# A transformer block on one core: pairs of score maxima moved between attention slots, gate products moved to slot 39

## Chip, cores and metric

The kernel runs on one core of a Trainium2 chip. The metric is the device time of one execution in microseconds (us); lower is better. Before the change the median of three runs is 2919.54 us.

## What is computed

The input is 8 images (batch entries) of 1024 tokens with 256 channels. Each goes through an attention part and a part with experts, both modulated by a vector per image:

```python
mod = (_silu(L0_c) @ L0_wmod).reshape(8, 6, 1, -1)
sa, ca, ga, sb, cb, gb = (mod[:, k] for k in range(6))      # gates ga, gb kept away from zero
h = _layernorm(x) * (1 + ca) + sa
x = x + ga * attn(h)     # 16 heads, causal, rope on 32 of 48 dimensions, output times W_o
h = _layernorm(x) * (1 + cb) + sb
x = x + gb * ffn(h)      # 16 experts of width 128 on 32-wide slices, top 2 of 16, then Wo and bo
```

In the attention, softmax of causal scores is taken for 16 heads; in the second part every token slice goes through all 16 experts and the gates of the top two weight their outputs, which are added and projected by Wo.

## The kernel before, in words

The work is written out by hand for each engine; instructions run in program order on each engine, and semaphores tie the engines together. An image has two stretches: 48 attention slots (`aslots`, index s), then 64 expert steps (`eslots`, index q). While an image attends, smaller pieces of work, called items, are put into its slots by `attend_slots`; while it goes through the experts, the first half of the next image's preparation is put into the steps by `expert_slots`.

A slot is one group of four heads g, one half c of the queries and one block j of 128 keys (`MAIN`). Heads go in two halves. PE (TensorE) computes scores of the first half, then the items of part 0 of the slot ("between"), then scores of the second half, then the items of parts 1 and 2 ("behind", "front"); at even slots it adds the product of weights and values of the two slots before (`values`). ScalarE takes the exponential of each half (L1393), and GpSimd masks the diagonal blocks (L1508). Scores of a half wait for the exponential two halves earlier. Slots on the diagonal are narrower: 512, 384, 256, 128 columns. In the second half of the queries four slots are full before those four. Slots 16 to 23 are diagonal ones of groups 2 and 3; 24 to 27, 32 to 35 and 40 to 43 are full.

Before the real scores of a group can be used, a maximum per row is needed. It comes from an item named ("pair", g, ...): two matmuls of up to 512 columns (L428, one for each half of the partitions; a masked pair is cut into four) into two PSUM banks, which VectorE reads with a masked maximum (L573, where the block lies on the diagonal) or a plain one (L576). There are 13 pairs for the second half of the queries of each group, 5 for the first. `rmax` (L582), `row` (transposed on PE at L500, copied by VectorE at L586) and a DMA of four issues on SyncE's queue (L780) carry the maximum to the queries of the group; the scores of a new group and half (slots 16, 20, 24, 32, 40) wait for it.

All items of PE write into a ring of three PSUM banks (`Ring`, banks 6, 7, 5): `ring_write` waits until the item that used the bank three uses before has been read. A pair takes two uses, a rope item, a group of transposes (`sums`, `tr`) or an output projection (`o`) takes one.

`PLACES` lists the places (slot, part) for the 47 pairs of a later image in order; slots 1, 2, 3, 5, 7 have one pair in part 0, from slot 9 to 36 an odd slot has one (part 0) and an even slot two (parts 0 and 1). The first image has its own list (`per_slot`). Eight rope items (rotary embedding of groups 2 and 3) lie in slots 0 and 2 to 8: VectorE shuffles (L607) and multiplies (L608), GpSimd multiplies and adds (L726, L739), SyncE moves the result to the queries and keys (L765).

In slot 22 VectorE forms the gated projections: `wog` = W_o times ga (two multiplications, L1474), `wfg` = Wo times gb (two, L1476), `bog` = bo times gb (L1478). The attention's output projection (`o`, L518, from slot 32 on) reads `wog` and waits for the semaphore d0_w. GpSimd adds `bog` to the residual at expert step 0; `wfg` is read by the last projection (`out`, L548) from expert step 36 on. The semaphore d0_w is cleared once an image.

Of the kernel before, what the change touches and what calls it, by code (L numbers as in the profile page):

```python
# [23 lines left out]
CH = C // P  # L24
# [312 lines left out]
PAIRS = [masked_pairs(0), [(((i, 0, pr),),) for i in range(4, 8) for pr in range(2)]]  # L337
# [74 lines left out]
def item_matmuls(pe, L, R, item):  # L412
# [57 lines left out]
    elif kind == "rope":  # L470
        g, isk, c = rope_of(item[1], R.alone)
        if g < 2:
            R.wait(pe, L, ("ht", c, CH - 1) if isk else ("qct", c))
        hd = slice(g * HG * RD, (g + 1) * HG * RD)
        if isk:
            for k in range(CH):
                mm = pe.matmul(out, L.wkr[:, k, hd], L.ht[:, k, half(c)], start=(k == 0), stop=(k == CH - 1))  # L477
        else:
            mm = pe.matmul(out, L.wqr[:, hd], L.qct[:, half(c)], start=True, stop=True)  # L479
    elif kind == "sum":  # L480
        R.wait(pe, L, ("kvt",))
        for t in range(4):
            mm = pe.matmul(out[:, 2 * t:2 * t + 2], L.kvsq[:, t * P:(t + 1) * P], L.halves[:, :], start=True, stop=True)
    elif kind == "qc":
        h, c = item[1:]
        R.wait(pe, L, ("qct", c))
        mm = pe.matmul(out, L.wqc[:, h * P:(h + 1) * P], L.qct[:, half(c)], start=True, stop=True)  # L487
    elif kind == "std":
        pe.wait_ge(S["f_ks"], 1)
        for t in range(4):  # L490
            for c in range(2):
                mm = pe.matmul(out[KVR * c:KVR * c + KVR, t * P:(t + 1) * P],
                               L.kstd[:, 4 * c + t:4 * c + t + 1].broadcast_to([P, KVR]), L.ident[:, :], start=True, stop=True)
    elif kind == "row":
        g, c = item[1:]
        if c:
            pe.wait_ge(S["c_mf"] if g else S["f_mf"], max(g, 1))
        else:
            R.wait(pe, L, ("pair", g, *PAIRS[0][-1]))
        mm = pe.transpose(out[0:4 * HG, 0:P], L.mxf if c else L.mx0[:, g, :], L.ident[:, :])  # L500
    elif kind == "sums":
        m = item[1]
        pe.wait_ge(S["c_o"], m + 1)
        for t in range(4):
            mm = pe.transpose(out[:, t * P:(t + 1) * P], L.ot[:, m % 2, t * P:(t + 1) * P], L.ident[:, :])  # L505
    elif kind == "tr":
        c, j = item[1:]
        R.wait(pe, L, ("sums", SEQ.index((NG - 1, c))))
        for t in range(4):
            mm = pe.transpose(out[:, t * P:(t + 1) * P], L.ao[:, 4 * c + t, j * P:(j + 1) * P], L.ident[:, :])  # L510
    elif kind == "o":
        c, n = item[1:]
        R.wait(pe, L, ("tr", c, CH - 1))
        if c == 0:
            pe.wait_ge(S["d0_w"], 5)
        for t in range(2):
            for k in range(CH):
                mm = pe.matmul(out[:, t * C:(t + 1) * C], L.at[:, k, (2 * n + t) * P:(2 * n + t + 1) * P], L.wog[:, k, :],  # L518
                               start=(k == 0), stop=(k == CH - 1))
    elif kind == "tr2":  # L520
        c, j = item[1:]
        pe.wait_ge(S[f"d{c}_xn"], 4)
        for t in range(4):
            mm = pe.transpose(out[:, t * P:(t + 1) * P], L.xn2[:, t, j * P:(j + 1) * P], L.ident[:, :])
    elif kind == "tm":
        c, j = item[1:]
        R.wait(pe, L, ("tr2", c, CH - 1))
        for k in range(CH):
            mm = pe.matmul(out, L.wms[:, k, j * P:(j + 1) * P], L.h2t[:, k, :], start=(k == 0), stop=(k == CH - 1))  # L529
    elif kind == "lg":  # L530
        c = item[1]
        R.wait(pe, L, ("tm", c, CH - 1))
        for t in range(4):
            for j in range(CH):
                o = t * P + j * 4 * NE
                mm = pe.matmul(out[:, o:o + 4 * NE], L.t32[:, j, t * P:(t + 1) * P], L.embd[:, :], start=True, stop=True)  # L536
    elif kind == "gt":
        c = item[1]
        pe.wait_ge(S[f"d{c}_r"], 17)
        for t in range(4):  # L540
            mm = pe.transpose(out[:, t * P:(t + 1) * P], L.eb[:, t * FH:(t + 1) * FH, :].rearrange("p a b -> p (a b)"),
                              L.ident[:, :])
    elif kind == "out":
        n = item[1]
        pe.wait_ge(S["e_add"], 30 * (n // 2 + 1))
        for t in range(2):
            for k in range(CH):
                mm = pe.matmul(out[:, t * C:(t + 1) * C], L.ct[:, k, (2 * n + t) * P:(2 * n + t + 1) * P], L.wfg[:, k, :],  # L548
                               start=(k == 0), stop=(k == CH - 1))
# [553 lines left out]

AHEAD = 2
EARLY = 3
PLACES = [(1, 0), (2, 0), (3, 0), (5, 0), (7, 0)]
PLACES += [(s, part) for s in range(9, 37) for part in range(2 - s % 2)]


def attend_slots(img):  # L1110


    slots = [([], [], []) for _ in range(NM)]
    if img:
        slots[1][1].extend([("out", 2), ("out", 3)])
        places = PLACES
        pairs = [("pair", 1, *p) for p in PAIRS[1][AHEAD:AHEAD + 5]]
        pairs += [("pair", g, *p) for g in (2, 3) for p in PAIRS[0]]
        pairs += [("pair", 1, *p) for p in PAIRS[1][AHEAD + 5:]]
        pairs += [("pair", g, *p) for g in (2, 3) for p in PAIRS[1]]  # L1120
    else:
        per_slot = [(0, 2), (1, 2), (2, 3), (3, 2), (4, 3), (5, 3), (8, 2), (9, 1), (10, 2), (11, 2), (12, 3), (13, 1), (14, 2), (15, 1),
                    (16, 2), (17, 2), (18, 2), (19, 1), (20, 2)] + [(s, 1 if s in (22, 23, 27, 29, 31, 33) else 2) for s in range(21, 37)]
        places = [(s, 2 * k // n) for s, n in per_slot for k in range(n)]
        early, second = [("pair", 0, *p) for p in PAIRS[1][EARLY:]], [("pair", 1, *p) for p in PAIRS[1]]
        pairs = early[:1] + [("pair", 1, *p) for p in PAIRS[0]] + early[1:]
        pairs += second[:5] + [("pair", 2, *p) for p in PAIRS[0]] + second[5:6] + [("pair", 3, *p) for p in PAIRS[0]] + second[6:]
        pairs += [("pair", g, *p) for g in (2, 3) for p in PAIRS[1]]
        slots[2][1].append(("row", 1, 0))
        slots[6][0].append(("rmax", 0))  # L1130
        slots[6][1].append(("row", 0, 1))
    assert len(places) == len(pairs)
    ropes = {s: ("rope", 8 + k) for k, s in enumerate((0, 2, 3, 4, 5, 6, 7, 8) if img else (3, 5, 6, 7, 8, 9, 10, 11))}
    for (s, part), pair in zip(places, pairs):
        if part and img and s and s in ropes:
            slots[s][1].append(ropes.pop(s))
        slots[s][part].append(pair)
    for s, rope in ropes.items():
        slots[s][1].append(rope)
    for s, g in ((21, 1), (29, 2), (37, 3)):  # L1140
        slots[s][0].insert(0, ("rmax", g))
    for s, row in ((13, (2, 0)), (17, (3, 0)), (21, (1, 1)), (29, (2, 1)), (37, (3, 1))):
        slots[s][2].append(("row", *row))
    for m, gc in enumerate(SEQ[:-1]):
        last = max(s for s, step in enumerate(MAIN) if step[:2] == gc)
        slots[last + 2][2].append(("sums", m))
    slots[27][1].append(("tr", 0, 0))
    slots[28][1].append(("tr", 0, 1))
    slots[32][1].append(("o", 0, 0))
    slots[33][1].extend([("o", 0, 1), ("stats", 0)])  # L1150
    slots[34][1].append(("xn", 0))
    slots[37][1].extend([("tr2", 0, 0), ("tr2", 0, 1)])
    slots[38][1].append(("tm", 0, 0))
    slots[39][1].extend([("tm", 0, 1), ("tlo", 0, 0)])
    slots[40][1].extend([("tlo", 0, 1), ("lg", 0), ("chain", 0, 1), ("chain", 0, 2)])
    slots[41][1].append(("exp", 0))
    for k in range(3, 18):
        slots[41 + (k - 3) // 3][1].append(("chain", 0, k))
    slots[46][2].append(("gt", 0))
    return slots  # L1160
# [68 lines left out]
def all_images(nc, L, O):  # L1229
# [18 lines left out]
    with nc.Block() as block:  # L1248
# [182 lines left out]
        def _(v):  # L1431
# [29 lines left out]
            for img in range(B):  # L1461
                for s, (between, behind, front) in enumerate(aslots[img]):
# [6 lines left out]
                    if s == 22:  # L1469
# [3 lines left out]
                        for k in range(CH):  # L1473
                            v.tensor_tensor(L.wog[:, k, :], L.wos[:, k, :], L.gate[:, 0, :],  # L1474
                                            ALU.mult).then_inc(S["d0_w"], 1)
                            v.tensor_tensor(L.wfg[:, k, :], L.wfs[:, k, :], L.gate[:, 1, :],  # L1476
                                            ALU.mult).then_inc(S["d0_w"], 1)
                        v.tensor_tensor(L.bog[:, :], L.bor[:, :], L.gate[:, 1, :], ALU.mult).then_inc(S["d0_w"], 1)  # L1478
# [214 lines left out]
```

## Time and profile before

| | us |
|---|---|
| runs of the kernel, median (lowest to highest) | 2919.54 (2918.32 to 2922.02) |
| the profiled execution, its own time | 2920.5 |
| its span, first to last instruction | 2918.1 |
| PE busy | 2816.6 |
| VectorE busy | 1863.0 |
| ScalarE busy | 1808.5 |
| GpSimd busy | 1246.2 |

The profile is one execution. PE is a matmul's stretch, PEld a weight load, DVE is VectorE, ACT ScalarE, POOL GpSimd, SPq the queue of DMA issues of SyncE. L428 is line 428 of the kernel. A busy time is the union of the instructions' stretches; matmuls overlap each other, so a stretch of matmuls is best read from start to start. "[0.45 <-DVE front L573]" behind an instruction tells that its engine was idle 0.45 us before it and that an update by VectorE's instruction of line 573 ended that.

### The profile page before, as it was taken

The numbers are of one execution on the slowest core, as the hardware profiler recorded it, in microseconds if no ns is written. First come the engines' busy times: TensorE is split into PE (matmuls) and PEld (weight loads), VectorE is DVE, ScalarE is ACT, GpSimd is POOL, SyncE is SP. The second block draws the span as 40 slices with busy tenths as digits, with TensorE's granted clock in tenths as the row PEclk, the third lists the DMA queues.
The fourth block names the chain that finished last, engine by engine and source line by source line (L and its number), as shares of the span: only waits on it lengthen the run. The fifth ranks groups of instructions, "written<-read, shape, count | busy, mean of one in ns | idle before, by whom it ended". The sixth has DMA issues, their size and how long they took to land.

```text
span 2918.1 us, 50109 instructions
## 1 busy us (share of the span) xinstructions
PE 2816.6 (97%) x16476; PEld 1241.9 (43%) x16476; DVE 1863.0 (64%) x4638; ACT 1808.5 (62%) x2148; POOL 1246.2 (43%) x1325
## 2 busy tenths in 40 slices
PE   7899999999999999999999999999999999999999
PEld 3344444444444443444444444444444444444433
DVE  5775666756666666666667666675756657667553
ACT  2346675566755677457675576655666566665687
POOL 4312645136451364414654146531565215561254
PEclk9899999999999999999999999999999999999999
DMA  6203453044430444304432055311453124530343
GB/s 156 57 5 99 118 130 73 1 108 122 120 71 8 119 118 107 71 21 121 122 97 61 23 134 130 87 47 46 121 133 89 32 71 119 124 88 20 77 127 94
DMA packets 176972, 252.96 MB, mean 87 GB/s; under 512 B 50509, under 2 KB 83293, under 8 KB 176621
## 3 DMA queue, kind: packets, MB, share of 16 engines
q1 hardware_dynamic: 176100, 248.44, 34.3%
q8 instruction: 136, 2.23, 0.3%
q10 hardware_dynamic: 620, 1.34, 0.2%
q14 instruction: 116, 0.95, 0.1%
HBM read 159.13 MB, written 12.63 MB: 59 GB/s over the span
## 4 chain that ended last, share of the span: by engine, by line
PE 86%; DVE 7%; issue 3%; ACT 2%; POOL 1%; SPq 1%; DMA 1%; ACTq 0%; DVEq 0%; POOLq 0%
PE ps L1279 17%; PE ps L1321 17%; PE ps L1339 16%; PE ps L1305 9%; PE ps L428 7%; PE ps L477 4%; PE ps L479 2%; PE ps L518 2%; PE ps L548 2%; DVE rest L573 1%; PE ps L529 1%; PE ps L505 1%; PE ps L536 1%; PE ps L463 1%; PE ps L487 1%
## 5 line engine op out<-in xcount | busy, mean ns | idle before, releaser
L1411 ACT ACTIVATE rest<-ps 128x1024 f32<-128x1024 f32 x1024 | 993.8, 1024 | 341.1 <-PE ps L1321 340.9
L1393 ACT ACTIVATE rest<-ps 128x1024 f32<-128x1024 f32 (+3 forms) x768 | 610.2, 809 | 537.4 <-PE ps L1279 511.6
L1518 POOL TENSOR_TENSOR rest<-rest 128x512 f32<-128x512 f32 x478 | 632.0, 1322 | 560.7 <-DVE rest L1448 548.1
L1448 DVE SCALAR_TENSOR_TENSOR rest<-ps,b2c,wide 128x512 f32<-128x512 f32 x512 | 384.0, 750 | 489.8 <-PE ps L1339 451.7
L1321 PE MATMUL ps<-wide,w1s 98*128 98x512 f32 x2048 | 655.1, 437 | 11.5 <-ACT rest L1411 8.7
L1339 PE MATMUL ps<-rest,w2s 128*32 128x512 f32 x4096 | 546.1, 605 | 0.6 <-ACT rest L1411 0.6
L1508 POOL TENSOR_SCALAR_AFFINE_SELECT rest<-rest 128x256 f32<-128x256 f32 x512 | 206.4, 411 | 772.3 <-ACT rest L1393 770.3
L573 DVE CUSTOM_DVE_ANT_0 rest<-ps,maskd 128x512 f32<-128x512 f32 (+3 forms) x1024 | 444.8, 487 | 118.8 <-PE ps L428 114.0
L1279 PE MATMUL ps<-wide 49*128 49x512 f32 (+3 forms) x2304 | 486.3, 511 | 10.2 <-ACT rest L1393 4.2
L1321 PEld LDWEIGHTS ps<-wide,w1s 98*128 98x128 f32 x2048 | 340.8, 188 | 301.0 <-ACT rest L1411 189.0
L576 DVE TENSOR_REDUCE front<-ps 128x1 f32<-128x512 f32 x512 | 329.0, 684 | 92.9 <-PE ps L428 88.7
L428 PE MATMUL ps<-wide 48*128 48x512 f32 (+3 forms) x1152 | 269.9, 500 | 37.8 <-DVE front L573 20.7
L1305 PE MATMUL ps<-rest,front 128*32 128x512 f32 (+3 forms) x3072 | 290.2, 496 | 0.0
L1279 PEld LDWEIGHTS ps<-wide 49*128 49x128 f32 x2304 | 195.5, 186 | 195.7 <-issue 121.3
L726 POOL TENSOR_TENSOR front<-front,sin 128x512 f32<-128x512 f32 x128 | 163.7, 1279 | 110.5 <-DVE front L607 110.2
L428 PEld LDWEIGHTS ps<-wide 48*128 48x128 f32 x1152 | 108.0, 187 | 219.1 <-DVE front L573 79.1
L1279 PE MATMUL ps<-heads 49*128 49x512 f32 (+3 forms) x768 | 168.0, 520 | 2.8 <-DMA heads<-front 2.6
L739 POOL TENSOR_TENSOR front<-front 128x512 f32<-128x512 f32 x128 | 163.0, 1273 | 10.0
L1339 PEld LDWEIGHTS ps<-rest,w2s 128*32 128x32 f32 x4096 | 80.6, 108 | 191.0 <-issue 189.5
L1305 PEld LDWEIGHTS ps<-rest,front 128*32 128x32 f32 x3072 | 80.7, 110 | 163.0 <-issue 113.5
L477 PE MATMUL ps<-front,wkr 128*128 128x512 f32 x256 | 125.5, 619 | 0.0
L1279 PEld LDWEIGHTS ps<-heads 49*128 49x128 f32 x768 | 66.7, 191 | 66.0 <-issue 43.8
(142 smaller groups left out, 2192.4 us busy)
## 6 DMA issues: line engine op xcount, KB each, us to landing
wide<-gate_rows SPq DMA_DIRECT2D x1024, 128.0 KB, 2.8
wide<-front SPq DMA_DIRECT2D x480, 64.0 KB, 2.0
wide<-front SPq DMA_DIRECT2D x192, 128.0 KB, 2.3
ao<-in_x SPq DMA_DIRECT2D x16, 512.0 KB, 5.1
heads<-front SPq DMA_DIRECT2D x64, 128.0 KB, 2.3
xs<-in_x SPq DMA_DIRECT2D x16, 512.0 KB, 5.0
out<-xs SPq DMA_DIRECT2D x32, 256.0 KB, 2.7
wide<-ao SPq DMA_DIRECT2D x96, 64.0 KB, 2.3
```

The costliest lines, as they stand in the source:

```text
L428: mm = pe.matmul(outs[hh][:, at:at + w], L.q2[g][rows, pr, i * P:(i + 1) * P].bitcast(F32R), L.k2[g][rows, pr, keys].bitcast(F32R), start= ...
L477: mm = pe.matmul(out, L.wkr[:, k, hd], L.ht[:, k, half(c)], start=(k == 0), stop=(k == CH - 1))
L573: ins = v.tensor_tensor_reduce(out=R.junk[hh][:, at:at + w], in0=src[:, at:at + w], in1=L.maskd[:, HALF - w:], scale=1.0, scalar=-3e38, op ...
L576: ins = v.tensor_reduce(dst, src[:, 0:w], AX.X, ALU.max)
L1279: mm = pe.matmul(bank(2 * (u % 2) + hh)[:, 0:HALF - f], L.k2[g][rows, pr, j * P:(j + 1) * P], L.q2[g][rows, pr, c * HALF + f:(c + 1) * HAL ...
L1305: mm = pe.matmul(bank(PVB)[h * VW:(h + 1) * VW, f:HALF], L.va[:, j, HG * g + h, :], L.pt[:, u % PTS, h % 2, f:HALF], start=(j == 0), stop= ...
L1321: mm = pe.matmul(bank(2 * (u % 2) + k), L.w1s[:, e, :], L.x2[:, c, 4 * j + 2 * p + k, :], start=True, stop=True)
L1339: mm = pe.matmul(bank(L2 + q % 2)[FD * h:FD * h + FD, :], L.w2s[:, e, :], L.hm[:, (2 * q + h // 2) % HM, (h % 2) * HALF:(h % 2 + 1) * HALF ...
L1393: nc.scalar.activation(L.pt[:, u % PTS, :, f:HALF], L.ps[:, 2 * (u % 2):2 * (u % 2) + 2, 0:HALF - f], ACT.Exp, scale=SCALE).then_inc(S["c_ ...
L1411: nc.scalar.activation(L.hm[:, u % HM, :], bank(2 * (u % 2), 2), ACT.Gelu).then_inc(S["e_gelu"], 1)
L1448: v.scalar_tensor_tensor(out=dst, in0=bank(L2 + q % 2), scalar=L.b2c[:, e:e + 1], in1=L.gb[:, q // 2 % GB, q % 2, :], op0=ALU.add, op1=ALU ...
L1518: g.tensor_tensor(dst, dst, L.gy[:, k % GY, :], ALU.add).then_inc(S["e_add"], 1)
```

## The change

Three things are changed. In the table of places for later images one pair less stands in slots 18, 22, 24 and 34 (each loses the one in part 1), and one more in slots 4 and 8 (part 0, where none stood) and in 27 and 35 (part 1, behind the one in part 0). So that the two new early places can be filled before the keys of group 2 are there, seven pairs of group 1 go first instead of five. The order of pairs within a group stays, the number is 47 as before. Second, three of the five gate multiplications (`wfg`, `bog`) move from slot 22 to behind the items of slot 39, for all images. Third, PE's wait before the first attention projection asks for two multiplications instead of five.

```diff
@@ -512,7 +512,7 @@
         if c == 0:
-            pe.wait_ge(S["d0_w"], 5)
+            pe.wait_ge(S["d0_w"], CH)
@@ -1103,8 +1103,9 @@
 AHEAD = 2
 EARLY = 3
-PLACES = [(1, 0), (2, 0), (3, 0), (5, 0), (7, 0)]
-PLACES += [(s, part) for s in range(9, 37) for part in range(2 - s % 2)]
+SOON = 7
+PLACES = [(s, 0) for s in (1, 2, 3, 4, 5, 7, 8)]
+PLACES += [(s, part) for s in range(9, 37) for part in range(2 - (s % 2 or s in (18, 22, 24, 34)) + (s in (27, 35)))]
@@ -1114,9 +1115,9 @@
-        pairs = [("pair", 1, *p) for p in PAIRS[1][AHEAD:AHEAD + 5]]
+        pairs = [("pair", 1, *p) for p in PAIRS[1][AHEAD:AHEAD + SOON]]
         pairs += [("pair", g, *p) for g in (2, 3) for p in PAIRS[0]]
-        pairs += [("pair", 1, *p) for p in PAIRS[1][AHEAD + 5:]]
+        pairs += [("pair", 1, *p) for p in PAIRS[1][AHEAD + SOON:]]
@@ -1473,6 +1474,8 @@
                         for k in range(CH):
                             v.tensor_tensor(L.wog[:, k, :], L.wos[:, k, :], L.gate[:, 0, :],
                                             ALU.mult).then_inc(S["d0_w"], 1)
+                    if s == 39:
+                        for k in range(CH):
                             v.tensor_tensor(L.wfg[:, k, :], L.wfs[:, k, :], L.gate[:, 1, :],
                                             ALU.mult).then_inc(S["d0_w"], 1)
                         v.tensor_tensor(L.bog[:, :], L.bor[:, :], L.gate[:, 1, :], ALU.mult).then_inc(S["d0_w"], 1)
```

## Rows read from the trace of the kernel before

**Rows 1.** The page: span, busy time of each engine, chain by engine.

```profile
span 2918.1 us, 50109 instructions
...
PE 2816.6 (97%) x16476; PEld 1241.9 (43%) x16476; DVE 1863.0 (64%) x4638; ACT 1808.5 (62%) x2148; POOL 1246.2 (43%) x1325
...
PE 86%; DVE 7%; issue 3%; ACT 2%; POOL 1%; SPq 1%; DMA 1%; ACTq 0%; DVEq 0%; POOLq 0%
```

**Rows 2.** Windows: window, length, busy per engine (count), clock, DMA; third image's attention.

```profile
807.50:968.50 161.00, 156.11 (x1018) 70.68 (x1018) 104.63 (x299) 85.88 (x112) 48.60 (x82) 1.00 0.19 44
```

**Rows 3.** Windows: slots 4, 17, 18, 21, 22, 24, 26, 27, 34, 35, 42.

```profile
823.78:828.40 4.62, 4.62 (x30) 1.78 (x29) 1.97 (x6) 1.94 (x2) 3.26 (x4) 1.00 0.28 70
867.93:870.45 2.52, 2.52 (x20) 1.39 (x16) 1.93 (x5) 2.07 (x3) 0.74 (x2) 1.00 0.00 0
870.45:874.34 3.89, 3.44 (x30) 1.52 (x29) 3.39 (x9) 1.33 (x3) 1.22 (x3) 1.00 0.01 2
878.83:881.48 2.65, 2.64 (x21) 1.48 (x18) 2.08 (x11) 2.15 (x3) 0.74 (x2) 1.00 0.03 6
881.48:885.41 3.93, 3.50 (x31) 1.62 (x31) 3.68 (x16) 1.26 (x3) 1.22 (x3) 1.00 0.02 4
886.48:890.60 4.12, 3.71 (x31) 1.50 (x31) 4.06 (x14) 2.36 (x3) 0.98 (x2) 1.00 0.00 0
893.34:897.87 4.53, 4.52 (x30) 1.52 (x29) 3.28 (x8) 2.60 (x3) 0.00 (x0) 1.00 0.00 0
897.87:900.61 2.74, 2.74 (x19) 1.30 (x15) 1.29 (x2) 1.49 (x2) 0.00 (x0) 1.00 0.00 0
922.96:928.38 5.42, 4.50 (x29) 1.51 (x29) 5.24 (x18) 2.05 (x2) 1.02 (x1) 1.00 0.00 0
928.38:930.63 2.25, 2.23 (x14) 0.88 (x10) 1.66 (x6) 1.02 (x1) 0.00 (x0) 1.00 0.00 0
952.23:956.00 3.77, 3.77 (x26) 1.10 (x25) 3.63 (x7) 3.06 (x4) 0.00 (x0) 1.00 0.40 94
```

**Rows 4.** Timeline, slot 18: start, us, engine, line, [idle before <-releaser].

```profile
872.03 0.69 DVE L573 CUSTOM_DVE_ANT_0 rest<-ps,maskd 128x512 f32<-128x512 f32 x1
...
872.26 0.50 PE L428 MATMUL ps<-wide 48*128 48x512 f32 x2 [0.45 <-DVE front L573]
```

**Rows 5.** Chain, slots 22 to 24: first and last gate piece of five, and next.

```profile
885.31 0.34 DVE rest L1474
...
886.65 0.54 DVE rest L1478
887.20 0.61 DVE front L576
```

**Rows 6.** Timeline, PE in slots 24, 26 and 27.

```profile
889.81 0.86 PE L1305 MATMUL ps<-rest,front 128*32 128x256 f32 x16
...
894.54 1.02 PE L1279 MATMUL ps<-wide 49*128 49x512 f32 x4
...
895.58 0.51 PE L428 MATMUL ps<-wide 48*128 48x512 f32 x2
...
896.01 1.92 PE L1305 MATMUL ps<-rest,front 128*32 128x512 f32 x16
...
899.07 1.02 PE L1279 MATMUL ps<-wide 49*128 49x512 f32 x4
...
900.02 0.66 PE L510 MATMUL ps<-ident,ao 128*128 128x128 f32 x4
```

**Rows 7.** Timeline, VectorE's first instruction after slot 39.

```profile
946.57 0.69 DVE L661 TENSOR_TENSOR front<-front 128x512 fp32r<-128x512 f32 x1 [3.51 <-ACT front L697]
```

**Rows 8.** Timeline, issues of the score row of slot 21.

```profile
881.75 2.42 SPq L780 DMA_DIRECT2D wide<-front  x4
```

**Rows 9.** The page, DMA issues: KB each, us from issue to landing.

```profile
wide<-front SPq DMA_DIRECT2D x480, 64.0 KB, 2.0
```

**Rows 10.** Timeline: load behind the last rope move; first pair of group 3.

```profile
848.06 1.19 SPq L1563 DMA_DIRECT2D xs<-in_x  x2
...
854.75 0.56 PE L428 MATMUL ps<-wide 48*128 48x128 f32 x4
```

## The prediction, made before the changed kernel ran

> **What bounds the kernel now.** I read the page first, then the attention stretch in windows, then single slots. The page gives TensorE (PE) 97% busy and 86% of the chain that ended last, VectorE 7% of that chain [rows 1]. So the end is set by the matmul queue, and whatever holds that queue for a moment is paid in full. The seven later images repeat each other: each has 48 attention slots in 161.0 us, and in the windows of all seven that length and PE's busy time agree within 0.1 us [rows 2]. I therefore cost one image (the third, from 807.5 us) and multiply by seven. In these 161.0 us PE is busy 156.1, so 4.9 us per image are plain idle time, and the granted clock there is 1.00, the level of 2.4 GHz [rows 2]. The windows by slot show where that idle time lies: slots 18, 22, 24 and 34 have 3.89-3.44 = 0.45, 3.93-3.50 = 0.43, 4.12-3.71 = 0.41 and 5.42-4.50 = 0.92 us, together 2.21 of 4.9; slots 4, 26, 27 have none to speak of [rows 3]. What ends it is VectorE: the second pair of slot 18 starts at 872.26 after 0.45 us idle that ended with L573, VectorE's masked maximum of the slot's first pair [rows 4]. A pair takes two of three PSUM banks, so the next pair must wait until VectorE has read the bank written three uses before. In slot 24 the pair waits behind more than that: the chain runs through the five gate multiplications, from 885.31 to the end of the last at 887.20, before the maximum that frees the bank [rows 5].
>
> **Price of a pair on PE.** The start-to-start times of the timeline give two prices [rows 6]. A second pair (behind both scores): in slot 26, scores at 894.54, pair at 895.58, values at 896.01, that is 1.47; the same scores without a second pair take 900.02-899.07 = 0.95; so 0.52. A first pair (between the two scores): in slot 27 scores, pair, scores take 900.02-897.87 = 2.15, where slot 27 starts at 897.87 [rows 3]; slot 42, with no pair, takes 3.77 in all, of which its two value groups of full width take what they take in slot 26, 897.87-896.01 = 1.86, leaving 1.91; so 0.24. A pair between the scores costs less than half of one behind them.
>
> **Part by part, one later image.**
> - Slot 18, second pair out: the idle 0.45 and the pair's 0.52 go: -0.97. What is late next is ScalarE's exponential of slot 17, already there before. Slot 22 likewise: -(0.43+0.52) = -0.95.
> - Slot 24: with one pair it is slot 27's 2.15 plus its own value groups, 890.60-889.81 = 0.79 [rows 3, 6], so 2.94 for 4.12: -1.18. More than 0.41+0.52, because here the first pair is held by the gate multiplications, and part of that hides in modelled matmul ends.
> - Slot 34: slot 42's 3.77 plus a first pair 0.24 is 4.01 for 5.42: -1.41.
> - Slot 21 now gets an unmasked pair where it had a masked one that held the transposes behind it. Slot 17, the same shape, takes 2.52 for 2.65 [rows 3]; between 0 and -0.13, I take -0.08, as VectorE still reads the pair just before.
> - Slots 4 and 8 get a first pair each: +0.24 each. VectorE has room: it is busy 1.97 of 4.62 us there [rows 3], a pair needs about 1.3 to 1.4 of it, and both sit ahead of that slot's rope item, whose data come later anyway. If that cover is gone, the rope turn on GpSimd (3.26 of 4.62 busy) is late, see the rivals.
> - Slot 27 gets a second pair: +0.52, and its first is now masked (a little longer on VectorE) with transposes behind the second, which wait for the first one's banks: I add 0.08. Lower bound 0.44 (the pair's own matmuls), upper bound the price it had in slot 34, 5.42-4.01 = 1.41. I take 0.60, as nothing else stands on VectorE in slots 26 and 27 (3.28 of 4.53 and 1.29 of 2.74 busy), which is slot 26's case, not slot 34's.
> - Slot 35 gets a second pair: +0.52, less the 0.10 by which it now waits for an exponential (2.25 against slot 27's 2.15): +0.42, same upper bound. Slot 36 then starts with VectorE still on that pair: +0.10, between 0 and 0.3.
> - Gates: two multiplications stay in slot 22 (0.34 each from start to start [rows 5]), three move behind slot 39's items. There VectorE is idle 3.51 us up to 946.57 [rows 7], and they need about 1.2. The first reader of what they write is GpSimd at the first expert step, eight slots on. The wait for two instead of five counts lets L518 go earlier, but it is passed long before slot 32. Hidden: 0.
> - Order within each group of heads is the same, so slots 16, 19, 20, 23, 25, 26, 28 to 33 keep their lengths, 0 +- 0.1 in all.
> - Score rows by DMA: a shorter slot 22 brings slot 24 forward to 881.48+(3.93-0.95)+1.07 = 885.53. Its row's four issues begin at 881.75 and last 2.42, the fourth starting near 883.6 [rows 8]; no row shows when these 2 KB writes land. Nearest, small writes on the same queue: 2.0 us [rows 9], so 885.6: a wait of 0.07. Below, 0; above, the old start 886.48, since it was met. Slot 20 has about 0.1 more room. I take 0.05.
> - The first image has its own table of places; only the gates move there, in a slot without a second pair: 0 to -0.3, I take 0.
>
> Sum: -0.97-0.95-1.18-1.41-0.08 = -4.59; +0.24+0.24+0.60+0.42+0.10+0.05 = +1.65; -2.94 an image, -20.6 us for seven. The profiled span 2918.1 becomes 2897.5 (the execution's own time 2920.5 becomes 2899.9, 2.4 of it outside the span); the median of the runs is 1.4 above the span, so 2919.5-20.6 = 2898.9 us.
>
> The 97% above could be read as "hardly anything to win". The Trainium skill, Perfetto Trace Analysis, Identifying the Most-Contended Engine, says that matmul busy time is a poor measure because matmuls are pipelined. The trace agrees: counted in idle time alone the four slots hold 2.21 us, counted from start to start 4.51. With idle time alone the sum would be 2.21 less the four added pairs' 1.55, seven times 0.7, near 2915 us.
>
> **Rivals.**
> 1. The stalls move instead of going: the second pairs in 27 and 35 are held as slot 34's was, 1.41 each. For: the same three banks, and VectorE busy 5.24 of 5.42 in slot 34. Against: that was slot 34's statistics and sums, which 27 and 35 do not have. Then +1.81 more, -1.1 an image: 2912.
> 2. The DMA of the score rows becomes the bound: slots 20 and 24 cannot start before they did. For: the margin is below 0.2 us by the nearest row. Against: it takes a landing of 2.9 us after the fourth issue. Then 0.97+0.95+0.08 are lost, -0.94 an image: 2913.
> 3. Slower: the pairs in slots 4 and 8 delay the rope items, hence GpSimd's turns, and the keys of head group 3 reach their place late; PE's first pair of that group, at 854.75 in slot 12, waits, with all behind it. In the trace the last of those issues is over by 848.06, when the next load starts on the queue [rows 10]; with about 2 us to land there are some 5 us of room. It decides from 5 us of lateness, and makes the kernel slower only from 8; 9 us would give +1 an image, 2927. Two pairs of 1.4 on VectorE can hardly give that.
> 4. The change does not do what it says: were the removed pairs' time not freed at all, slower by seven times 1.6; the rows of slot 18 speak against it, since the idle time before the pair ends with VectorE's read and nothing else.
>
> **How the numbers follow.** Forecast 0.84, rival 1 0.06, rival 2 0.05, rivals 3 and 4 together 0.03, a mixture near no change 0.02. The forecast's own bounds are -3.5 (slot 27 at its lower end, no DMA wait, slot 21 at -0.13, small gains in the first image and in slots 16 to 33) and -2.0 an image (one of the two added second pairs held for most of its 0.9 more): 2895 to 2906. Rivals 1 and 2 lie above that and are left out, 0.14 with the others, and a little at the ends. Measurement tells this kernel from no change at about 0.2%, 5.8 us, or 0.83 an image; all cases but the last two pass it. Faster 0.94, same 0.03, slower 0.03.
>
> **What would show it.** Per later image the attention stretch should fall from 161.0 to about 158.1 and the expert stretch stay. Slots 18 and 22 near 2.9 to 3.0, slot 24 near 2.95, slot 34 near 4.0; slots 4 and 8 near 4.86, 27 near 3.35, 35 near 2.67. The gate multiplications L1476 and L1478 lie in slot 39 without a wait behind them. Wrong would be: idle time of PE before the second pair in 27 or 35; the first score of slot 24 released by a DMA; a first pair in slot 4 that costs 0.5; or a slot 12 that waits for the rope move.

## The result, and the profile after

The changed kernel takes 2896.7 us, the median of five runs (2896.62 to 2899.86), against 2919.54 for the kernel before (five runs, 2916.97 to 2922.02); the ratio is 0.9924, 95% interval 0.991 to 0.9939. The forecast was 2898.9 in a range of 2895.0 to 2906.0, faster with a chance of 0.94. The profiled execution of the changed kernel is its slowest run: 2899.86 us, with a span of 2898.0. The page has the same counts of instructions as before, and a chain in which VectorE's share has gone from 7% to 5% [rows 1].

```profile
span 2898.0 us, 50109 instructions
...
PE 2809.7 (97%) x16476; PEld 1241.3 (43%) x16476; DVE 1864.4 (64%) x4638; ACT 1811.2 (62%) x2148; POOL 1248.8 (43%) x1325
...
PE 87%; DVE 5%; issue 3%; ACT 2%; POOL 1%; SPq 1%; DMA 1%; ACTq 0%; DVEq 0%; POOLq 0%
```

The windows of the third image show where the time went (same columns as [rows 2, 3]). First its whole attention stretch, then slots 4, 18, 21, 22, 24, 27, 34, 35 and 36.

```profile
808.40:966.45 158.05, 155.24 (x1018) 70.69 (x1018) 104.71 (x299) 86.15 (x112) 48.79 (x82) 1.00 0.19 45
...
824.63:829.49 4.86, 4.86 (x32) 1.98 (x31) 3.25 (x8) 2.05 (x2) 3.27 (x4) 1.00 0.31 80
871.84:874.78 2.94, 2.94 (x28) 1.30 (x27) 2.08 (x5) 1.33 (x3) 1.23 (x3) 1.00 0.01 2
879.31:881.82 2.51, 2.51 (x19) 1.39 (x15) 2.19 (x10) 2.06 (x3) 0.71 (x2) 1.00 0.03 7
881.82:884.82 3.00, 3.00 (x30) 1.40 (x29) 2.77 (x13) 1.34 (x3) 1.23 (x3) 1.00 0.02 5
885.88:888.83 2.95, 2.95 (x28) 1.41 (x29) 2.45 (x10) 2.02 (x3) 0.74 (x2) 1.00 0.00 0
896.10:899.45 3.35, 3.32 (x20) 1.52 (x16) 1.91 (x5) 2.05 (x2) 0.00 (x0) 1.00 0.00 0
921.82:925.83 4.01, 4.01 (x27) 1.30 (x26) 3.87 (x16) 2.05 (x2) 1.02 (x1) 1.00 0.00 0
925.83:928.38 2.55, 2.54 (x17) 1.21 (x15) 2.04 (x5) 1.30 (x2) 0.00 (x0) 1.00 0.00 0
928.38:933.05 4.67, 4.67 (x30) 1.40 (x26) 4.21 (x10) 2.80 (x3) 0.82 (x2) 1.00 0.00 0
```

Slots 18, 22, 24 and 34 now have their whole length as PE's busy time; the idle 0.45, 0.43, 0.41 and 0.92 us of before are gone. The table has the medians over the seven later images.

| slot | before, us | after, us | difference | forecast |
|---|---|---|---|---|
| 4, 8 (each) | 4.62 | 4.86 | +0.24 | +0.24 |
| 18 | 3.89 | 2.94 | -0.95 | -0.97 |
| 20 | 3.42 | 3.47 | +0.05 | 0 |
| 21 | 2.65 | 2.52 | -0.13 | -0.08 |
| 22 | 3.93 | 2.99 | -0.94 | -0.95 |
| 24 | 4.12 | 2.95 | -1.17 | -1.18 |
| 27 | 2.74 | 3.35 | +0.61 | +0.60 |
| 34 | 5.42 | 4.01 | -1.41 | -1.41 |
| 35 | 2.25 | 2.54 | +0.29 | +0.42 |
| 36 | 4.50 | 4.67 | +0.17 | +0.10 |

Together with hundredths elsewhere the attention stretch is 3.02 us shorter in each later image (161.00 to 157.98; forecast 2.94), the expert stretches between them keep their 194.45 us. Seven times 3.02 is 21.1; the spans differ by 20.1. The missing 1.0 us is not in the later images' attention or in the expert stretches between them, but in the first image's attention, the last expert stretch and the start. The rows of the changed kernel for the first two:

```profile
61.20:261.40 200.20, 175.10 (x1039) 77.10 (x1039) 130.64 (x382) 85.72 (x111) 49.03 (x81) 0.89 0.18 41
...
2728.60:2898.00 169.40, 160.31 (x880) 64.39 (x880) 78.08 (x110) 132.48 (x140) 82.98 (x63) 1.00 0.45 117
```

Before, the same two took 195.6 us at a granted clock of 0.91 and 172.3 us at 0.98, and the first began at 62.0 instead of 61.2 us. So the first image was 4.6 longer at a lower clock, the last stretch 2.9 shorter at 1.00, the start 0.8 shorter. A clock below 1.00 is a part of the stretch at 1.2 GHz instead of 2.4. Over all profiled kernels of this study but one the first image took 194.4 to 200.2 us, and over all of them the last expert stretch 169.4 to 174.0, with no relation to the edit that could be seen. (The exception is the kernel with half reads below, whose edit reaches the first image too: 187.8 us.) The times of one kernel scatter by 3 to 8 us (thirteen runs of the kernel before: 2914.86 to 2921.13), while a later image of the kernel before repeats within 0.02 us and one of the changed kernel within 0.12. The comparisons below are made per later image where they can be.

### The profile page after: what moved, and what is told of

Its sections match the earlier page's. It is cut to its first block, busy times and chain, and to the rows that moved or that the text cites. A ratio compares the mean times of both kernels' runs of the same rounds, so it can differ in the third digit from the quotient of the medians.

```text
span 2898.0 us, 50109 instructions
## 1 busy us (share of the span) xinstructions
PE 2809.7 (97%) x16476; PEld 1241.3 (43%) x16476; DVE 1864.4 (64%) x4638; ACT 1811.2 (62%) x2148; POOL 1248.8 (43%) x1325
## 4 chain that ended last, share of the span: by engine, by line
PE 87%; DVE 5%; issue 3%; ACT 2%; POOL 1%; SPq 1%; DMA 1%; ACTq 0%; DVEq 0%; POOLq 0%
PE ps L1280 18%; PE ps L1322 17%; PE ps L1340 16%; PE ps L1306 9%; PE ps L428 7%; PE ps L477 4%; PE ps L479 2%; PE ps L548 2%; PE ps L518 2%; PE ps L529 1%; PE ps L505 1%; PE ps L536 1%; PE ps L463 1%; PE ps L487 1%; DVE rest L1449 1%
```

## Experiments

Prices below are medians over the seven later images, from windows of the same kind, and "an image" is the sum of the slots' medians. In the diffs the lines with a minus are those of the kernel that was edited; "..." stands for lines left out. A kernel that ran once only has no interval; its windows still hold seven later images.

**The gate products alone.** Places of before, gates as changed.

```diff
-SOON = 7
-PLACES = [(s, 0) for s in (1, 2, 3, 4, 5, 7, 8)]
-PLACES += [(s, part) for s in range(9, 37) for part in range(2 - (s % 2 or s in (18, 22, 24, 34)) + (s in (27, 35)))]
+SOON = 5
+PLACES = [(1, 0), (2, 0), (3, 0), (5, 0), (7, 0)]
+PLACES += [(s, part) for s in range(9, 37) for part in range(2 - s % 2)]
```

> The kernel before with the three gate multiplications (wfg, bog) moved from slot 22 to slot 39 and the places of the pairs left as they were. Theory A (the stalls come from the ring of three banks behind VectorE, and each slot can be priced alone): only slot 24 changes. VectorE is through with the two wog multiplications 1.2 us earlier, the first pair of slot 24 finds its banks free, and slot 24 takes 3.5 us instead of 4.12; slots 18, 22 and 34 keep 3.89, 3.93 and 5.42. That is -0.6 us a later image, -4 us in all, about 2915. Rival B (the gate work on VectorE is most of the gain, the places add little): slots 22 and 24 fall to about 3.0 each, -2 us an image, -14 us in all, about 2905.

Ten runs gave 2916.68 against 2917.89 us for the kernel before, ratio 0.9996 (0.9986 to 1.0005). Only slot 24 changed, 4.12 to 3.51, and an image got 0.60 shorter, as expected. Its window:

```profile
885.33:888.84 3.51, 3.44 (x31) 1.62 (x31) 3.12 (x12) 2.36 (x3) 0.74 (x2) 1.00 0.00 0
```

Seven times 0.6 is 4.2 us, less than the scatter of single runs; the windows see it, the whole time does not tell it from nothing. The window confirms that the three products sat ahead of the reads on which slot 24's pairs wait [rows 5].

**The places alone.** Everything as changed, but all five products in slot 22.

```diff
-                    if s == 39:
+                    if s == 22:
```

> The changed kernel with all five gate multiplications back in slot 22. Theory A: slots 18, 22, 34 as in the changed kernel (2.94, 2.99, 4.01); VectorE ends the gate work 4.3 us after the start of slot 22, that is 1.3 us into slot 23, so the pair of slot 23 is read 0.55 us later, the first pair of slot 24 waits a little and slot 24 takes about 3.05 to 3.15 instead of 2.95. Gain 2.9 us an image instead of 3.0, about 2898. So gates alone and places alone add up to more than both together. Rival B: the gate work holds slot 24 at about 4.1 and slot 23 with it, and 1.2 us an image of the gain are lost, about 2905.

2898.6 us, ratio 0.9935 (0.9919 to 0.9952), -3.01 an image: the same as the whole change. The expected loss did not come. Slot 24 is as short as with the gates moved:

```profile
883.26:886.20 2.94, 2.94 (x28) 1.29 (x28) 2.77 (x11) 2.01 (x3) 0.78 (x2) 1.00 0.00 0
```

The first pair does start later, 0.85 us into the slot instead of 0.54 in the changed kernel, as the products still stand before the reads. But from its start to the second scores it then takes 0.32 instead of 0.64, and these begin 1.17 us into the slot, no later than the 1.18 of the changed kernel:

```profile
884.11 0.51 PE L428 MATMUL ps<-wide 48*128 48x256 f32 x4
...
884.43 1.06 PE L1280 MATMUL ps<-wide 49*128 49x512 f32 x4
```

With one pair in the slot, a first pair that is this late is absorbed. So the two parts do not add: alone the gates are worth 0.60 and the places 3.01, together 3.02. Moving the gate products is worth nothing in this kernel once slot 24's second pair is gone.

**One pair from slot 34 to slot 35, nothing else.**

```diff
-PLACES += [(s, part) for s in range(9, 37) for part in range(2 - s % 2)]
+PLACES += [(s, part) for s in range(9, 37) for part in range(2 - (s % 2 or s == 34) + (s == 35))]
```

> The kernel before with one move alone: the second pair of slot 34 goes to slot 35. Theory A: slot 34 falls from 5.42 to 4.01, slot 35 rises from 2.25 to 2.54 and slot 36 from 4.50 to 4.68; nothing else changes. -0.94 us a later image, -6.6 us in all, span about 2911. Rival C (the vector engine's total work in slots 34 to 36 sets their length, wherever the pair stands): the three slots keep their sum of 12.17 and the span stays at 2918.

One run: 2910.98 us, -0.96 an image where -0.94 was expected. Slots 34, 35 and 36:

```profile
921.28:925.28 4.00, 4.00 (x27) 1.29 (x26) 3.86 (x16) 2.05 (x2) 1.02 (x1) 1.00 0.00 0
925.28:927.82 2.54, 2.53 (x16) 1.21 (x14) 2.04 (x5) 1.29 (x2) 0.00 (x0) 1.00 0.00 0
927.82:932.50 4.68, 4.68 (x31) 1.40 (x27) 4.22 (x10) 2.81 (x3) 0.82 (x2) 1.00 0.00 0
```

This one move carries its own third of the gain, and the pair that lost 1.41 in slot 34 costs 0.29 + 0.17 = 0.46 in its new place. For this pair rival 1, stalls that move along, is false; for the one moved to slot 27 the window of the changed kernel says the same (+0.61, not 1.41).

**What a second pair's 0.52 consists of.** In the kernel before, VectorE reads only the first 256 of 512 columns of each pair that is unmasked or lies in a single block, and so leaves the other half of the keys out of these maxima. PE's instructions and their order are unchanged.

```diff
+                r = HALF // 2 if w == HALF and R.rope0 else w
...
-                    ins = v.tensor_tensor_reduce(out=R.junk[hh][:, at:at + w], in0=src[:, at:at + w], in1=L.maskd[:, HALF - w:], scale=1.0,
+                    ins = v.tensor_tensor_reduce(out=R.junk[hh][:, at:at + r], in0=src[:, at:at + r], in1=L.maskd[:, HALF - r:], scale=1.0,
...
-                    ins = v.tensor_reduce(dst, src[:, 0:w], AX.X, ALU.max)
+                    ins = v.tensor_reduce(dst, src[:, 0:r], AX.X, ALU.max)
```

> The kernel before, in which VectorE reads only the first 256 of the 512 columns of an unmasked or single-block pair in the later ring of every image (the maxima over the other half of the keys are left out). PE's instructions and their order are the same; such a read takes about 0.42 us instead of 0.69. Theory A (the bank read by VectorE holds the second pair): slot 18 from 3.89 to 3.62, slot 22 from 3.93 to 3.66, slot 34 from 5.42 to 5.15, slot 24 from 4.12 to about 3.5, each by the 0.27 us that the read of the first bank is shorter (slot 24 by two such reads before it). Rival D (a second pair costs PE itself more, by its weight loads or the change between forms of matmul, and VectorE's update only happens to come then): the slots keep their lengths. Only the stalls can change: slots 26 and 27, where the second pair or none is held, keep 4.53 and 2.74.

2885.87 us in one run, -3.41 an image. The two reads of a pair fell from 1.29 to 0.76 us, 0.27 each, and slots 18, 22 and 34 fell by 0.27 each as expected (slots 18, 24, 26 and 34 below; before in [rows 3]). But slot 24 fell by 0.27 too, where 0.6 was expected, and slots that should have stood still did not: 12, 16, 20 and 36 by 0.26, 28, 32 and 30 by 0.34, 0.31 and 0.21, 17 by 0.14, and slot 26 from 4.52 to 4.25, though PE was shown busy for all but 0.01 us of it [rows 3].

```profile
857.75:861.37 3.62, 3.45 (x30) 1.52 (x29) 2.21 (x8) 1.47 (x3) 1.22 (x3) 1.00 0.01 2
872.98:876.83 3.85, 3.71 (x30) 1.50 (x30) 3.52 (x14) 2.37 (x3) 0.98 (x2) 1.00 0.00 0
879.58:883.83 4.25, 4.25 (x30) 1.51 (x29) 2.22 (x8) 2.60 (x3) 0.00 (x0) 1.00 0.00 0
908.05:913.20 5.15, 4.50 (x30) 1.51 (x29) 4.71 (x20) 2.05 (x2) 1.02 (x1) 1.00 0.00 0
```

The timeline of slot 26 with half reads shows where the 0.27 was; PE's partners of before are in [rows 6].

```profile
880.78 1.02 PE L1280 MATMUL ps<-wide 49*128 49x512 f32 x4
881.55 0.49 PE L428 MATMUL ps<-wide 48*128 48x512 f32 x2
881.97 1.92 PE L1306 MATMUL ps<-rest,front 128*32 128x512 f32 x16
...
880.97 0.76 DVE L577 TENSOR_REDUCE front<-ps 128x1 f32<-128x256 f32 x2 [0.57 <-PE ps L428]
```

VectorE's two reads of the first pair in the kernel before:

```profile
894.74 1.29 DVE L576 TENSOR_REDUCE front<-ps 128x1 f32<-128x512 f32 x2 [0.57 <-PE ps L428]
```

Before, the second pair started 895.58 - 894.54 = 1.04 us after the scores ahead of it; now it starts 881.55 - 880.78 = 0.77 after them. In both, that is some 0.2 us after VectorE's first read ends (880.97 and half of 0.76, 881.35, here; 894.74 and half of 1.29, 895.38, before). The time was a wait for the bank, and no idle time was shown, because the scores' stretch of 1.02 us covers it: here that stretch would end at 881.80, 0.25 after the pair behind it began. The Trainium skill, Perfetto Trace Analysis, Tensor Engine Instruction, says that a matmul's end in the profile is computed and not observed; this row agrees, and shows what follows from it: a wait of up to a quarter of a microsecond leaves no gap.

So the 0.52 of the second pair in slot 26 was at least 0.27 of waiting for VectorE. Even with the shorter read the pair still starts 0.2 us after that read ends, so the 0.25 that is left is an upper bound for its matmuls; it is about what a first pair costs (0.24). Of the other even slots with a second pair, 10 and 14 kept their length; the rest fell by 0.21 to 0.34.

**Following that further: pairs into slot 6.** If a first pair costs 0.24 and a second pair in 14 and 30 still 1.0 and 0.87, slots 14 and 30 should be emptied as well, into slots 6 and 25.

```diff
-SOON = 7
-PLACES = [(s, 0) for s in (1, 2, 3, 4, 5, 7, 8)]
-PLACES += [(s, part) for s in range(9, 37) for part in range(2 - (s % 2 or s in (18, 22, 24, 34)) + (s in (27, 35)))]
+SOON = 8
+PLACES = [(s, 0) for s in range(1, 9)]
+PLACES += [(s, part) for s in range(9, 37) for part in range(2 - (s % 2 or s in (14, 18, 22, 24, 30, 34)) + (s in (25, 27, 35)))]
```

> The changed kernel with two more moves by the same prices: a first pair in slot 6 (none there) for the second pair of slot 14, and a second pair in slot 25 for that of slot 30; eight pairs of the first group go ahead. Theory A: slot 6 +0.24, slot 14 from 4.37 to about 3.3 (its second pair is held by VectorE for 0.6 and costs 0.43 itself), slot 25 +0.6, slot 30 from 4.26 to about 3.25. Together -1.2 us a later image against the changed kernel, -8 us in all, about 2889. Rival C: what is freed in slots 14 and 30 comes back as waits in the next narrow slots or, since slot 6 lies among the rope items with GpSimd nearly full, as a late rope move at slots 9 to 12: no change against the changed kernel, 2897.

2900.47 us, ratio 0.9943 (0.9928 to 0.9958), so not better than the change. Slots 14 and 30 fell to 3.37, by 1.00 and 0.86, and 25 rose by 0.59, as expected. Slot 6 rose from 3.76 to 4.69, by 0.93 instead of 0.24, and slot 15 by 0.13 in the median, as slot 16 behind it waits for its score row (in three of the seven images by 0.5 to 0.8). Slot 6, with what the pair waits for:

```profile
827.02:831.71 4.69, 4.27 (x30) 1.56 (x29) 4.17 (x9) 1.19 (x2) 4.24 (x6) 1.00 0.51 112
...
827.32 0.68 DVE L608 TENSOR_TENSOR front<-ps,cos 128x512 f32<-128x512 f32 x1
828.15 0.50 PE L428 MATMUL ps<-wide 48*128 48x512 f32 x2 [0.42 <-DVE front L608]
```

The pair's second bank is still held by the rope item of slot 5, whose multiplication ends at 828.00; the transposes of slot 5 took the use between them. A place in the ring costs what the item three uses before makes of it, not what the slot looks like.

**The same with slot 6's pair behind the scores.**

```diff
-PLACES = [(s, 0) for s in range(1, 9)]
+PLACES = [(1, 0), (2, 0), (3, 0), (4, 0), (5, 0), (6, 1), (7, 0), (8, 0)]
```

> The changed kernel with the moves out of slots 14 and 30 again (one into slot 25), but the early pair in slot 6 stands behind the rope item instead of between the scores. Between the scores it cost 0.93 us, since its second bank is the one that VectorE reads for slot 5's rope item until 0.98 us into slot 6. Theory A: behind, at about 2.1 us, that bank is long free and it costs its plain price, slot 6 from 3.76 to about 4.25; slot 14 to 3.37, slot 15 to 1.2 (the row of slot 13 now lands after slot 16 could start), slot 25 to 3.33 and slot 30 to 3.37 as in the run before. -0.6 us a later image against the changed kernel, about 2893. Rival C: GpSimd's rope work or the rows take it back, 2897.

2896.79 us, ratio 0.9924 (0.9907 to 0.9941). Slot 6 came to 4.18, +0.42 over 3.76:

```profile
833.27:837.45 4.18, 4.18 (x29) 1.58 (x28) 3.51 (x9) 1.08 (x2) 3.88 (x6) 1.00 0.57 125
```

The medians of the slots add up to -0.60 an image against the change, as expected, but the attention stretches of its images now vary from 157.33 to 158.18, with a mean of only -0.34 an image, or 2.4 us in all. The whole time cannot be told from the change's, and the 2893 us expected were not reached. What varies is slot 15: 1.17 to 1.22 us in four images, 1.60, 1.95 and 2.02 in the fifth, sixth and eighth, where it was 1.07 before slot 14 was emptied. The first scores of slot 16 show why, in the fourth image and in the eighth:

```profile
1217.80 0.70 PE L1280 MATMUL ps<-wide 49*128 49x512 f32 x2 [0.24 <-DMA wide<-front]
...
2627.01 0.70 PE L1280 MATMUL ps<-wide 49*128 49x512 f32 x2 [1.07 <-DMA wide<-front]
```

In all seven images it is the row's DMA that releases them. Its issues ended at 1216.71 and at 2625.09 (2.53 and 2.54 us for four), so the scores began 1.09 us behind them in the one image and 1.92 in the other. The room that this row had is used up, as the expectation's rival C said of the rows, and from here on its landing time, which differs from image to image, sets the pace. Why it differs was not found.

**The margin of the score rows.** Two extra small issues on SyncE's queue ahead of the rows for slots 20 and 24, in the changed kernel and in the one before.

```diff
...
+                    if img and (g, c) in ((3, 0), (1, 1)):
+                        for d in range(2):
+                            sp.dma_start(L.idle[4 * img + 2 * c + d:4 * img + 2 * c + d + 1, :], L.neg1[:, :]).then_inc(L.s_idle, 16)
...
```

> The changed kernel with two small extra DMA issues on the queue ahead of the score rows made in slots 17 and 21 of the later images, so that both rows land about 1.2 us later. Theory A with the margin as I read it (row landed 0.2 to 0.4 us before slots 20 and 24 start): the time between the starts of slots 18 and 20 grows by about 0.85 us and that from 22 to 24 by about 1.0, some +1.85 us an image, +13 us in all, and the first scores of both slots are released by the DMA. If the margin were wide, as for a row that is not near the bound, nothing changes.

> The same two extra issues in the kernel before. There slots 20 and 24 start 1.3 and 1.1 us after their rows have landed: nothing at slot 20, at most +0.1 us at slot 24, less than 1 us in all. Together with the run beside it this tells how much of the DMA's cover the change has used up.

One run each. Changed kernel: 2901.28 us, +0.51 an image: slot 19 1.07 to 1.33, slot 23 1.07 to 1.25, slot 20 +0.03. (In two of the seven images slot 15 or slot 19 took another 0.28 or 0.36.) Kernel before: 2922.51, +0.01 an image. That was the point: before the change, these rows had room for the delay, after it they have not. The loss is smaller than the expected 1.85 because two issues of one row to DRAM took only 0.54 and 0.51 us, where four of the rows' own take 2.44 (kernel with delayed rows; the queue, then PE):

```profile
868.51 0.54 SPq L1633 DMA_DIRECT2D idle_rows<-neg  x2
869.10 2.44 SPq L782 DMA_DIRECT2D wide<-front  x4
...
878.81 0.51 SPq L1633 DMA_DIRECT2D idle_rows<-neg  x2
879.36 2.44 SPq L782 DMA_DIRECT2D wide<-front  x4
...
872.62 0.70 PE L1282 MATMUL ps<-wide 49*128 49x512 f32 x2 [0.38 <-DMA wide<-front]
882.88 0.70 PE L1282 MATMUL ps<-wide 49*128 49x512 f32 x2 [0.29 <-DMA wide<-front]
```

The first scores of slots 20 and 24 are now released by the DMA. With delays of 0.59 us (868.51 to 869.10) and 0.55 us (878.81 to 879.36) the slots came 0.26 and 0.18 late, so in the change the row of slot 20 has some 0.33 us to spare and that of slot 24 0.37. Before, it was at least the whole delay. Rival 2 was false, but by a third of a microsecond. It is also the limit of this way: a change that takes much more out of slots 18 to 22 gains nothing there without an earlier row, as slots 14 and 15 showed above.

**Second pairs behind the values.** If half of a second pair's price is waiting, PE could do the slot's products of weights and values first. In the changed kernel the second pairs of slots 10, 12, 16, 26, 27, 28, 32, 35 and 36 go behind them (`late`), and then those of 14, 20 and 30 as well.

```diff
...
-        slots[s][part].append(pair)
+        slots[s][3 if img and part and s not in (14, 20, 30) else part].append(pair)
...
+                    for item in late:
+                        item_matmuls(pe, L, RA[img], item)
```

> The changed kernel in which the second pair of slots 10, 12, 16, 26, 27, 28, 32, 35 and 36 of the later images stands behind the slot's value products (in the odd slots behind its other items) instead of before them; slots 14, 20 and 30 keep theirs. Theory A2 (formed after the half-read run: the 0.52 us of a second pair is 0.25 of matmuls and 0.27 of waiting for VectorE's read of the first pair, hidden in modelled matmul ends): behind the values the first pair has been read, so each of these slots loses up to 0.27 us, slots 16, 26, 36 from 3.43, 4.53, 4.67 to about 3.2, 4.25, 4.4; part of it may come back as a later first pair in the next slot, since that now waits for the moved one. Between -0.8 and -2.4 us a later image, about 2885. Rival D2 (0.52 is what a pair costs PE wherever it stands alone behind scores): no slot changes by more than 0.05, 2897.

> The same with slots 14, 20 and 30 as well. Theory A2: slot 14 loses the 0.6 us by which its second pair is held now, slot 30 likewise, but slots 15 and 31 behind them are the narrow ones of 128 columns, whose pair comes 0.25 us after the slot's start and must wait about 0.45 us for VectorE; slot 21's maximum and the score row of slot 24 come later after slot 20's move. Net -0.3 to +0.3 us an image against the run beside it. Rival D2: no change against the changed kernel.

Both were slower than the change per image, where a gain was expected of the first: 2901.59 us, ratio 0.994 (0.9923 to 0.9956), +0.51 an image; and 2901.72 in one run, +0.61 an image (0.10 more than the first, within the 0.3 expected). Most slots whose pair was moved did fall: slot 26 from 4.53 to 4.35, 10 by 0.26, 32 by 0.23, 16 and 36 by 0.14, 28 by 0.07, while 12 and 35 did not; in the second kernel 14 from 4.37 to 3.68 and 30 from 4.23 to 3.55. The next pairs then wait instead: slot 13 from 1.99 to 2.46, 17 from 2.52 to 2.88, 29 from 1.93 to 2.32, 33 from 4.52 to 4.94, and in the second 15 and 31 by 0.51 and 0.55, 21 by 0.48. Slots 26, 29 and 33 with nine moved:

```profile
891.14:895.49 4.35, 4.35 (x29) 1.60 (x30) 1.99 (x6) 2.61 (x3) 0.00 (x0) 1.00 0.00 0
903.90:906.22 2.32, 2.10 (x14) 0.83 (x10) 2.13 (x5) 0.91 (x2) 0.41 (x1) 1.00 0.00 0
916.71:921.63 4.92, 4.67 (x26) 2.67 (x22) 3.40 (x13) 2.42 (x3) 0.00 (x0) 1.00 0.02 5
```

With all twelve moved, the timeline of slot 15 has the pair moved out of slot 14, VectorE's read of it, and the wait of slot 15's own pair for that read:

```profile
860.81 0.50 PE L428 MATMUL ps<-wide 48*128 48x512 f32 x2
...
861.34 0.69 DVE L573 CUSTOM_DVE_ANT_0 rest<-ps,maskd 128x512 f32<-128x512 f32 x1 [1.06 <-PE ps L428]
...
862.19 0.50 PE L428 MATMUL ps<-wide 48*128 48x512 f32 x2 [0.66 <-DVE front L573]
```

A pair that starts later is also read later, and the next slot's first pair needs those banks. As these rows read, what counts is the distance from pair to pair on VectorE, and the change gains where this does not because it leaves more room between pairs, in 18, 22, 24 and 34. That is a reading of the rows; no run varied the distance alone.

## Why the prediction was right, step by step

- **The bound.** Right, and confirmed by the experiments: every slot's change came out of the matmul queue and was paid in full, and shorter reads on VectorE with no change to PE made the kernel 31 us faster (one run against a median of 2917.15; 23.9 of it in the later images, and the first image was 7.8 shorter in the profiles). Costing one later image and multiplying by seven was good to 0.08 us an image.
- **Slots 18, 22, 24, 34.** -4.47 measured for -4.51. The idle time before the pair and the pair's own 0.52 both went, and nothing else came late in its place. For slot 24 the reason given, that its first pair is held by the gate products and that part of this hides in modelled ends, was right (0.60 with the gates alone) but incomplete: with one pair left the delay costs nothing even if the products stay.
- **The prices 0.52 and 0.24.** Right as prices, and they carried the sum. The prediction took 0.52 for what the pair itself takes on PE. The half reads showed that 0.27 of it is a wait for VectorE that no idle time shows. The idle time of slot 26, "none to speak of", was right as a number but not as a sign that nothing is waited for, and the 0.44 taken as "the pair's own matmuls" was no lower bound for a price: with half reads the pair of slot 26 added 0.25. Neither did harm here, since the prices are start-to-start differences and have the wait in them.
- **Slots 4, 8, 27.** +0.24, +0.24, +0.61 for +0.24, +0.24, +0.60. Rope items and GpSimd had the cover that was assumed. Slot 6, which was not used, would have cost 0.93: slots 4 and 8 were cheap by their neighbours in the ring, which the prediction's argument (VectorE's busy share) did not look at.
- **Slots 35 and 36.** +0.29 and +0.17 for +0.42 and +0.10. The step that was mis-sized is the split: 0.13 less in the one, 0.07 more in the other, 0.46 for 0.52 together.
- **Slot 21** reached the lower end of its bound, -0.13 for -0.08. **The score rows** cost 0 in slot 24 for a taken 0.05; slot 20 took 0.05 more for a taken 0. The row of slot 24 lands about 0.37 us before it is needed, so the landing time of 2.0 us taken from the nearest row [rows 9], whose transfers are of 64 KB and not small, was some 0.4 too long. In the third image the profile names the row's DMA at the weights of slot 24's first scores, which the prediction had set down as a sign of being wrong. The same place in the kernel before stands second:

```profile
885.85 0.33 PEld L1280 LDWEIGHTS ps<-wide 49*128 49x128 f32 x4 [0.28 <-DMA wide<-front]
...
886.45 0.33 PEld L1279 LDWEIGHTS ps<-wide 49*128 49x128 f32 x4 [0.28 <-issue]
```

The idle time is the same 0.28 us and slot 23 keeps its 1.07, so the row landed shortly before it was needed and held nothing.
- **Gates.** The product pieces lie in slot 39 (VectorE, changed kernel) and the next instruction on VectorE waits another 2.30 us, so they are hidden:

```profile
940.89 0.76 DVE L1479 TENSOR_TENSOR rest<-wfs,gate 128x256 f32<-128x256 f32 x2
...
941.56 0.62 DVE L1481 TENSOR_TENSOR rest<-bor,gate 128x256 f32<-128x256 f32 x1
...
944.48 0.69 DVE L661 TENSOR_TENSOR front<-front 128x512 fp32r<-128x512 f32 x1 [2.30 <-ACT front L697]
```

- **The total.** Forecast 2898.9, measured 2896.7: 0.6 us of the difference is the 0.08 an image, the rest lies within the scatter of the runs, a part of which is the clock. That the profiled execution came out at 2899.86 where 2899.9 was forecast is partly chance: 21.1 us gained and 1.0 given back by stretches that the change does not touch.
- **The rivals.** 1 (stalls move) was excluded by the slot windows and the single move; 2 (score rows) by slots 19 and 23, which kept their 1.07, with a margin that the delayed rows measured; 3 (rope chain) and 4 (nothing freed) by the windows: slot 12 took 4.58 us for 4.57, and the four slots fell.
- **The sum from idle time alone.** It took 1.55 for the four added pairs, which come to 0.24 + 0.24 + 0.60 + 0.42 = 1.50; that moves its 2915 us by 0.4.

## What to carry to other kernels

Cost a matmul item from start to start in two places that differ by that item alone, not from PE's idle time; here the prices held where the item was moved to a place with like neighbours in its ring of banks (slots 4, 8, 27), and not in slot 6. Gains of two edits that relieve the same wait do not add, so measure each alone and both together. And a place freed early uses up the room of whatever arrives there by DMA: know that margin before going on. Here it was a third of a microsecond at slots 20 and 24, and less than the 1.00 us that emptying slot 14 took out ahead of slot 16.

## What the runs showed of the hardware

- PE's busy time hides waits of up to about 0.27 us, as the second pair of slot 26 shows: the slot was busy 4.52 of 4.53 us and still got 0.27 shorter when only VectorE's reads were shortened (half reads).
- A first pair that starts 0.3 us late can cost nothing: in slot 24 of the kernel with the places alone it took 0.32 us from its start to the second scores, in the changed kernel 0.64, and the second scores began 1.17 and 1.18 us into the slot.
- Two issues of one row to DRAM took 0.51 us of SyncE's queue, four of a score row 2.44, that is 0.26 against 0.61 each. The scores that waited for such a row began 1.1 us behind the end of its issues as a rule, and up to 1.9 us in the kernel with slot 6's pair behind.
- GpSimd's two masks in slot 39 took 1.02 us beside the gate products, 0.77 before the change. The Trainium skill, SBUF — State Buffer, SBUF: two separate sides, says that a GpSimd instruction that reads SBUF and a VectorE instruction with two SBUF inputs exclude each other on a shared pair of ports. The rows agree in direction: in the kernel before, the two masks of slot 23 ran beside these products and took 1.06 us, and 0.87 in the changed kernel, where VectorE read PSUM beside them. Nobody waited for the 0.25 in slot 39, which kept its 2.56 us. Slot 39, the changed kernel first:

```profile
941.44 1.02 POOL L1511 TENSOR_SCALAR_AFFINE_SELECT rest<-rest 128x256 f32<-128x256 f32 x2 [3.45 <-ACT rest L1394]
...
943.52 0.77 POOL L1508 TENSOR_SCALAR_AFFINE_SELECT rest<-rest 128x256 f32<-128x256 f32 x2 [3.45 <-ACT rest L1393]
```

- The opening image ran partly at 1.2 GHz (granted clock 0.91 before, 0.89 after), the last expert stretch too in the kernel before (0.98) but not in the changed one (1.00), while from the second image to the eighth's attention the clock was 1.00 in both. Their lengths differ from run to run, 194.4 to 200.2 us and 169.4 to 174.0. Nothing that was tried here tells why.
